# A graph kernel whose mean layers multiply by whole edge counts: rows scaled by their degree, one adjacency part instead of two

## The reference, cut to what matters

```python
cnt = segment_sum(ones, tgt); inv_cnt = 1.0 / maximum(cnt, 1.0)
for i in range(3):                       # the three mean layers with a norm
    x_in = x
    agg = segment_sum(x[src], tgt) * inv_cnt[:, None]
    h = agg @ W_l[i].T + x @ W_r[i].T + b[i]
    h = (h - mean(h)) * rsqrt(var(h) + 1e-5) * ln_g[i] + ln_b[i]
    x = relu(h) + x_in
...
h = agg / maximum(deg, 1.0)[:, None] @ W_l + b + x @ W_r      # the last mean layer
out = layernorm(x + h * sigmoid(h))
```

## Time and profile before

| | |
|---|---|
| median of 3 runs | 1023.49 us (1018.66 to 1024.08) |
| profiled execution | 1026.04 us, span from first to last instruction 1024.3 us |
| PE busy | 875.0 us (85%) |
| DVE busy | 692.1 us (68%) |
| ACT busy | 499.2 us (49%) |
| POOL busy | 333.7 us (33%) |
| mean layers 0 to 2 in the span | about 287 to 470 us |
| last mean layer and end | about 945 to 1024 us |

### The profile page before, as it was taken

How to read it: one execution, slowest core, us unless ns; L and a number is a source line. 1 busy time by engine, 2 the same in 40 slices (tenths; PEclk the granted TensorE clock), 3 DMA queues, 4 the chain that set the end, 5 groups by cost and what they waited for, 6 DMA issues and landing times.

```text
span 1024.3 us, 13343 instructions
## 1 busy us (share of the span) xinstructions
PE 875.0 (85%) x3642; PEld 624.8 (61%) x3642; DVE 692.1 (68%) x1228; ACT 499.2 (49%) x966; POOL 333.7 (33%) x286
## 2 busy tenths in 40 slices
PE   3979768678969999974999998999999988999793
PEld 2666245456747777753666765676655865667572
DVE  7997635576964646476887577964898569875414
ACT  2386004344534313345775566754776467743421
POOL 3000724567011123335360255503652064502100
PEclk9989557898969999996999999999999999999897
DMA  4413525878314130414683177812886058721001
GB/s 104 143 32 95 140 77 164 247 206 273 132 42 173 40 114 0 135 62 107 164 202 86 37 180 188 218 42 64 187 221 191 4 142 217 196 55 42 1 1 50
DMA packets 58198, 122.16 MB, mean 119 GB/s; under 512 B 8025, under 2 KB 21627, under 8 KB 58134
## 3 DMA queue, kind: packets, MB, share of 16 engines
q0 software_dynamic: 20048, 52.18, 21.5%
q1 hardware_dynamic: 35061, 63.82, 20.2%
q10 hardware_dynamic: 3024, 5.31, 1.4%
HBM read 105.56 MB, written 15.73 MB: 118 GB/s over the span
## 4 chain that ended last, share of the span: by engine, by line
PE 71%; DVE 16%; ACT 5%; issue 4%; DMA 1%; another core or an unknown queue 1%; SPq 0%; DVEq 0%; ACTq 0%
PE ps L908 14%; PE ps L653 12%; PE ps L885 10%; PE ps L924 6%; PE ps L940 6%; PE ps L847 5%; PE ps L796 5%; PE ps L772 4%; PE ps L755 2%; DVE z_parts L1581 2%; ACT slot_recs L995 2%; PE ps L744 1%; PE ps L645 1%; PE ps L659 1%; PE ps L679 1%
## 5 line engine op out<-in xcount | busy, mean ns | idle before, releaser
L908 PE MATMUL ps<-z_parts,onehot_dst 128*125 128x512 f32 x664 | 207.5, 418 | 12.6 <-DVE z_parts L1581 9.5
L653 PE MATMUL ps<-w,xT 128*125 128x512 f32 x660 | 175.0, 419 | 12.7 <-DVE w L1224 4.9
L1581 DVE SCALAR_TENSOR_TENSOR z_parts<-ps,z_parts 128x512 fp32r<-128x512 f32 x216 | 147.6, 687 | 50.8 <-ACT z_parts L1124 43.3
L1124 ACT ACTIVATE z_parts<-ps 128x512 fp32r<-128x512 f32 x216 | 129.1, 598 | 87.5 <-PE ps L885 78.1
L885 PE MATMUL ps<-x_parts,gather_lhs 128*128 x432 | 143.9, 419 | 32.1 <-DVE x_parts L1558 21.0
L908 PEld LDWEIGHTS ps<-z_parts,onehot_dst 128*125 128x125 f32 x664 | 111.6, 188 | 81.4 <-issue 63.0
L653 PEld LDWEIGHTS ps<-w,xT 128*125 128x125 f32 x660 | 126.5, 197 | 49.2 <-issue 19.9
L604 POOL DMA_INDIRECT gathered<-rel_rows,rowi x83 | 88.6, 1068 | 161.3 <-DMA rel_rows<-x_cur 96.1
L619 POOL DMA_INDIRECT queued<-node_rows,srci x60 | 96.1, 1601 | 104.0 <-ACT queued L1058 88.2
L885 PEld LDWEIGHTS ps<-x_parts,gather_lhs 128*128 128x128 f32 x432 | 81.4, 195 | 65.8 <-issue 48.9
L584 POOL TENSOR_TENSOR w<-w_stage,w 128x512 fp32r<-128x512 f32 x36 | 47.9, 1360 | 179.4 <-ACT w L957 179.4
(11 more groups left out here) (240 smaller groups left out, 1204.1 us busy)
## 6 DMA issues: line engine op xcount, KB each, us to landing
w_stage<-in_weights SPq DMA_DIRECT2D x22, 1024.0 KB
onehot_dst<-onehot_rows SPq DMA_DIRECT2D x80, 250.0 KB
onehot_rows<-onehot_dst ACTq DMA_DIRECT2D x20, 250.0 KB
gather_lhs<-edge_src_rows SPq DMA_DIRECT2D x8, 432.0 KB, 8.6
node_rows<-work SPq DMA_DIRECT2D x20, 160.0 KB, 2.0
queued<-node_rows,srci POOLq DMA_INDIRECT x116
node_rows<-work SPq DMA_DIRECT2D x20, 90.0 KB, 2.0
rel_rows<-rel_rows_out SPq DMA_DIRECT2D x10, 160.0 KB, 1.9
```

The lines of the kernel that those rows point to most:

```text
L653: mm = pe.matmul(ps[0:R, bank, :], lt[:, a, k, n * R:(n + 1) * R], w[:, b, k, :], start=first and k == 0 and (a, b) == THREE[0], stop=last ...
L908: mm = pe.matmul(ps[0:R, d, :], S[:, j // SK % SR, j % SK, :], Z[:, g % ZR, a, :], start=False, stop=False, skip_group_check=True)
L1124: nc.scalar.activation(Z[:, g % ZR, HI, :], of, ACT.Relu).then_inc(z_hi, 1)
L1581: v.scalar_tensor_tensor(out=Z[:, g % ZR, LO, :], in0=of, scalar=0.0, in1=Z[:, g % ZR, HI, :].bitcast(F32), op0=ALU.max, op1=ALU.subtract) ...
```

## The change

The mean layers are computed times their degree. With d the degree of a row (at least 1), d * h = counts @ (x W_l) + (d * x) W_r + d * b.

- **Counts stay whole numbers.** The kernel takes them as exact in the high part up to 4096, so `mean_tile` has two products per source tile instead of three: 10 instead of 15. The multiplication of the counts by the reciprocal is gone.
- **Two blocks keep a low part.** At most 2 of the 25 blocks of 125 by 125 can hold a count above 4096. DVE, PE and ACT look for the largest entry of each block (`block_max`, `block_row`, a chain of 13 small DVE operations), PE copies the low parts of the two blocks found, from an address in a register, to `CLO` (`low_blocks`), and each mean layer adds two products with them, with source and destination tile from registers (`mean_low`).
- **x is multiplied by its degree** on ACT ahead of the transposes (`by_degree`, one per tile, rows of `x_cur` into `work`, counted by `xd_made`). The rows `x @ W_l` come out multiplied too, so `y_high` and `y_low` take the reciprocal as a factor. The roots take `eps * d^2`.
- **The bias** is multiplied by the degree: five products with four rows of degree parts (`DGR`, `deg_rows` in the trace) behind all `z_tile`s (`z_bias`), instead of one with two rows of ones ahead of each.
- **Degrees** are summed to one column per tile (25 products of one column instead of 10 of 313 or 312), and `deg_made` comes within the second round of DVE's first norm.
- **Places.** `DGR` shares its memory with the rows `WEB`, so SP stores it, waits for the third layer's `z_bias`, then loads `WEB` (`web_load(0)`) and only then weight 13 (`w_load(13)`); the first five `queue_set`s move behind `w_highs(9 + 2 * l)` on ACT.

```diff
@@ PE @@
             def x_tile(l, n):
-                pe.wait_ge(x_made, XM_MEAN[l] + n + 1)
-                transposes(n, X[0:R, n, :])
+                pe.wait_ge(xd_made, NT * l + n + 1)
+                transposes(n, H[0:R, n, :])
...
             def z_tile(l, n):
-                bias(n, k)
-                mm = natural(n, XT, W[1], n, first=False, last=False)
+                mm = natural(n, XT, W[1], n, last=False)
...
+            def z_bias(l):
+                k = l if l < NL1 else NL1 + NL2
+                pe.wait_ge(bias_in[k % 2], 32 * (k // 2 + 1))
+                if l == NL1:
+                    pe.wait_ge(dgr_in, 16)
+                else:
+                    pe.wait_ge(dgr_made, 1)
+                for n in range(NT):
+                    mm = pe.matmul(ps[0:R, n, :], DGR[:, n * R:(n + 1) * R], BIAS[:, k % 2, :],
+                                   start=False, stop=False)
+                mm.then_inc(zb_done, 1)
...
+            def low_blocks():
+                pe.wait_ge(low_made, 3)
+                pe.wait_ge(at_made, NT)
+                for j in range(2):
+                    wd = low_word(j)
+                    b = field(wd, 6, 31, NB - 1)
+                    mm = pe.matmul(ps[0:R, 5, P * (j + 1):P * (j + 1) + R], ident[0:R, 0:R],
+                                   ATL[0:R, bass.ds(b * R, R)], start=True, stop=True)
+                mm.then_inc(low_done, 1)
...
+            def mean_low(l):
+                if l == 0:
+                    pe.wait_ge(clo_made, 1)
+                pe.wait_ge(y_out, Y_L1[l] + NT)
+                for j in range(2):
+                    wd = low_word(j)
+                    s = field(wd, 0, 7, NT - 1)
+                    d = field(wd, 3, 7, NT - 1)
+                    pe.matmul(psf[0:R, bass.ds(d * D, D)], CLO[0:R, j, :], XS[0:R, HI, bass.ds(s, 1), :],
+                              start=False, stop=False, skip_group_check=True)
+
             def mean_tile(l, n):
...
                 for s in range(NT):
-                    for a, b in THREE:
-                        mm = pe.matmul(ps[0:R, n, :], AT[0:R, a, s, n * R:(n + 1) * R], XS[0:R, b, s, :],
-                                       start=False, stop=s == NT - 1 and (a, b) == THREE[-1])
+                    for b in (HI, LO):
+                        mm = pe.matmul(ps[0:R, n, :], AT[0:R, HI, s, n * R:(n + 1) * R], XS[0:R, b, s, :],
+                                       start=False, stop=s == NT - 1 and b == LO)
                 mm.then_inc(o_done, 1)
...
                 for n in range(NT):
                     z_tile(l, n)
+                    if l == 0 and n < NT - 1:
+                        (lambda: None, deg_rows, block_max, block_row)[n]()
+                    if l == 0 and n == NT - 2:
+                        low_blocks()
+                z_bias(l)
+                mean_low(l)
@@ ACT @@
+            def by_degree(n, count):
+                act.wait_ge(x_made, count)
+                nc.scalar.activation(H[0:R, n, :], X[0:R, n, :], ACT.Copy, scale=degp[0:R, n:n + 1])\
+                    .then_inc(xd_made, 1)
...
                 if l == 0:
                     for s in range(NT):
-                        act.wait_ge(an_made, s + 1)
                         nc.scalar.copy(AT[:, HI, s, :], TC[:, s, :]).then_inc(at_hi, 1)
...
+                    act.wait_ge(low_done, 3)
+                    nc.scalar.copy(CLO[0:R, :, :], ps[0:R, 5, P:3 * P].rearrange("p (j n) -> p j n", n=P)[:, :, 0:R])\
+                        .then_inc(clo_made, 1)
                 w_highs(8 + 2 * l)
+                act.wait_ge(z_done, l + 1)
+                w_highs(9 + 2 * l)
                 if l == NL1 - 1:
                     for k in range(0, EARLY, 2):
                         queue_set(0, k)
-                act.wait_ge(z_done, l + 1)
-                w_highs(9 + 2 * l)
                 if l < NL1 - 1:
-                    for n in range(NT + 1):
+                    for n in range(NT + 2):
                         if n < NT:
-                            root(n, NT * (l + 1) + n + 1)
+                            root(n, NT * (l + 1) + n + 1, epsd)
                             normal(H[0:R, n, :], ps[0:R, n, :], n, NT * (l + 1) + n + 1, h_made)
-                        if n >= 3:
+                        if n >= 2:
+                            by_degree(n - 2, XM_L1[l + 1] + n - 1)
+                        if 3 <= n <= NT:
                             tr_high(n - 3, XT, n - 3, TR_L1[l + 1] + n - 2)
@@ SP @@
+            sp.wait_ge(dgr_made, 1)
+            sp.dma_start(dg_d, DGR[:, :].bitcast(F32)).then_inc(dgr_out, 16)
+            sp.wait_ge(zb_done, NL1)
+            sp.wait_ge(dgr_out, 16)
+            web_load(0)
             w_load(13)
```

More of the change, by code:

```diff
@@ L418, in bias_load @@
             def bias_load(k, row):
-                sp.dma_start(BIAS[:, k % 2, :].bitcast(F32), rw_d[:, row, :]).then_inc(bias_in[k % 2], 16)
+                for i in (0, 2):
+                    sp.dma_start(BIAS[i:i + 2, k % 2, :].bitcast(F32), rw_d[:, row, :]).then_inc(bias_in[k % 2], 16)
             def ln_load(l):
@@ new lines, in deg_rows, with block_max @@
+            def deg_rows():
+                pe.wait_ge(y_out, 4)
+                for n in range(NT):
+                    mm = pe.transpose(ps[0:4, 7, n * R:(n + 1) * R] if n < 4 else ps[0:4, 5, 0:R],
+                                      DG4[0:R, n, :], ident[0:R, 0:R])
+                mm.then_inc(dgr_tr, 1)
+            def block_max():
+                pe.wait_ge(y_out, NT)
+                pe.wait_ge(low_made, 1)
+                pe.transpose(ps[0:NB, 6, 0:R], bm[0:R, :], ident[0:R, 0:R]).then_inc(low_done, 1)
@@ L961, in w_highs, with root @@
                     w_high(j, k)
-            def root(n, count):
+            def root(n, count, eps=None):
                 act.wait_ge(ln_var, count)
-                nc.scalar.activation(sd[0:R, n:n + 1], mv[0:R, n, 1:2], ACT.Sqrt, bias=epst[0:R, 0:1])\
+                nc.scalar.activation(sd[0:R, n:n + 1], mv[0:R, n, 1:2], ACT.Sqrt,
+                                     bias=epst[0:R, 0:1] if eps is None else eps[0:R, n:n + 1])\
                     .then_inc(ln_sd, 1)
@@ L974, in y_high @@
                 act.wait_ge(y_done, NREL * NT + count)
-                nc.scalar.copy(XS[0:R, HI, n, :], ps[0:R, bank, :]).then_inc(y_hi, 1)
+                nc.scalar.activation(XS[0:R, HI, n, :], ps[0:R, bank, :], ACT.Copy, scale=rdegp[0:R, n:n + 1])\
+                    .then_inc(y_hi, 1)
+            def by_degree(n, count):
+                act.wait_ge(x_made, count)
+                nc.scalar.activation(H[0:R, n, :], X[0:R, n, :], ACT.Copy, scale=degp[0:R, n:n + 1])\
+                    .then_inc(xd_made, 1)
             act.wait_ge(edges_in, 64)
@@ L1047, in _ @@
                     normal(X[0:R, n - 1, :], H[0:R, n - 1, :], n - 1, n, x_made)
+                    act.wait_ge(deg_made, 1)
+                    by_degree(n - 1, n)
                 if 2 <= n < NT:
@@ L1167, in _ @@
                 normal(X[0:R, n, :], H[0:R, n, :], n, NT * (NL1 + 2) + n + 1, x_made)
+                by_degree(n, XM_L3 + n + 1)
                 if n >= 2:
@@ L1177, in _ @@
                 act.wait_ge(o_done, NT * NL1 + n + 1)
-                nc.scalar.activation(X[0:R, n, :], ps[0:R, n, :], ACT.Sigmoid).then_inc(sg_out, 1)
+                nc.scalar.activation(X[0:R, n, :], ps[0:R, n, :], ACT.Sigmoid, scale=rdegp[0:R, n:n + 1])\
+                    .then_inc(sg_out, 1)
             for n in range(NT):
```

124 lines of the change are left out of this document (93 added, 31 removed).

## The result

The changed kernel takes **1053.55 us** as a median of 4 runs (1051.44 to 1056.19), the kernel before 1023.78 beside it: ratio 1.0288, 95% interval [1.0235, 1.0340]. The forecast was 1057, with a range of 1036 to 1070. The profiled execution took 1051.44 us with a span of 1049.6, 25.3 longer than that of before; PE is busy 859.7 us instead of 875.0, DVE 692.3 and ACT 515.9. So PE has 15 us less work and the program takes longer: the time went into waits.

The account below looks back on a forecast made before the run. The prediction took PE's in-order path from a layer's first root to the next layer's first product as the bound, not the products. Its terms, 1.2 + 1 + 9.4 + 11.3 + 10.1 + 4 - 3.6 = +33.4, gave 1057 us, range 1036 to 1070.

Parts of the forecast that it names:

- What bounds it: Layer 0: PE and DVE nearly level from tile 2; PE's 13.9 us from first root to next layer's first product matters.
- Head of layer 0, +1: Before layer 0's z tiles: degree sums, small DVE operations and by_degree cost more than the saved reciprocal wait; +1 us (-3 to +5).
- Search and weight 9, +9.4: Layer 0, z tiles to first root: the block search delays w_highs(8) and weight 9's load; root at 31.0, +9.4 us.
- The ring, +11.3 and +10.1: Layers 0 and 1: x_tile(n - 2) waits on tile n's products through DVE and ACT, closing a chain; +11.3 and +10.1 us.
- my 4: Layers 0 and 1: loss per layer from PE's lower clock after waits, 4 us taken between bounds 0 and 8.6.
- Layer 2, +4: Layer 2: weight 13 loads only after z_bias, delaying ACT's queue_sets and root; +4 us.
- Last mean layer, -3.6: Last mean layer: by_degree adds 0.9 us, but fewer products let tile 4 start earlier at the end; -3.6 us.
- z_bias and mean_low, +1.2 over the layers: Mean layers: z_bias saves about 1.0 us a layer, mean_low adds 1.4; +0.4 each, +1.2 for three layers.
- products bound it: Rival: PE sets the pace throughout, so cutting products makes the kernel faster, 1002 us; chance 7 in 100.
- every burst is cold: Rival: every product burst runs at the lower clock, 1066 us, or 1070 with a colder block search; chance 15 in 100.
- the search and weight 9 hide: Rival: only the loops, layer 2 and the tail count and the clock stays full; about 1040 us, chance 15 in 100.
- gains and losses cancel: Rival: one closed loop costs less and the search hides; within 5 us of 1023, chance 5 in 100.

Follow-up runs that it names:

- the cut alone: The kernel before with two products per source tile instead of three in all four mean layers, nothing else changed: 981.35 us, ratio 0.9924.
- the version that hides the search: The kernel with the three edits, with layer 0's head reordered and the block search moved into existing waits: 978.34 us, ratio 0.9859 to the kernel before.
- the head's reordering: The kernel with the three edits, with DVE's statistics of tiles 0 to 3 ahead of its degree wait and transpose copies one round later: 980.22 us, ratio 0.9887.
- closed alone in the kernel before: The kernel before, with PE in layers 0 and 1 waiting for tile n's normal ahead of tile n - 2's transposes: 1012.78 us, ratio 1.0237.
- the kernel with weight 13 early: The changed kernel, with SP issuing weight 13's load ahead of its wait for the third z_bias: 1052.74 us, ratio 1.0328 to the kernel before.
- the opened kernels: Changed kernels with by_degree of tile n - 2 ahead of root and normal of tile n in layers 0 and 1; that edit alone: 1030.47 us, ratio 1.0105.
- the kernel with the three edits: The changed kernel with by_degree ahead of root and normal, weight 8's split and low_blocks reordered, weight 13 loaded early: 1015.9 us, ratio 0.9981.

## Why the prediction was right, by its steps

- **What bounds it.** "A shorter product tile can pay little there" held: the cut alone is worth 7.5 us in the total and 11.0 by stages, of 23.1.
- **Head of layer 0, +1.** Measured +0.1, which is partly luck. The degree products went from 7.2 to 9.3 us, +2.1 where I took +2.3. But the first y tile came 7.1 us later (22.7 behind the first b_self product, before 15.6), where my added terms make 5.2, and 7.0 were made up between it and the z tiles, where I took 4.46: the second y tile now ran in 3.02 us instead of 5.32. The head also hid a cost that I did not see as one. Its rounds, 5.35 us from root to root (4.54 before), are themselves a ring, and reordering them was worth 6.4.
- **Search and weight 9, +9.4.** Measured +9.2; the root came at 30.8 for 31.0. The chain was as worked out: z tile 4 and `w_highs(8)` behind the search, then the load (ACT waited 8.85). But when that order was undone 5 to 6.5 came back, not 9.4. The rest stays with the added products on PE, which in the version that hides the search doesn't wait for DVE there and still needs 19.0 from the z tiles to the adjacency products, 16.7 before. Counted from b_self, that version's products start 4.0 us sooner than before, the head's reordering included.
- **The ring, +11.3 and +10.1.** Measured +11.8 and +10.1. Shown from both sides: opened, it gives 12.9 instead of 25.4; closed alone in the kernel before, it costs 13.7 and 10.7. Of the two parts in layer 1, the 21.2 us at full clock are 25.4 - 4.1 = 21.3. The clock's part is mis-sized: my 4 stood for two bursts, their transposes and the y tile together, and those lost 4.1 up to y and 1.5 in the y tile, 5.6. The bound of 8.6, every burst at 0.50 from end to end, was not reached, since only one of a layer's two bursts ran so. The Trainium skill, page "TensorE: Matmul & The Clock Gate", section "HAM oscillation — how this bites in real kernels", says that in a loop of short bursts with waits between them each burst starts at the lower clock. This trace agrees, more than I allowed for: in both layers each burst and the y tile began at 0.50, the first behind waits of 8.13 and 4.70 us, the others behind 3.40. Layer 0's first rounds hold one more part that I did not have: from the root to the statistics of tile 2 it took 5.3 us (4.4 in layer 1, 4.25 forecast). There POOL's work on the late weight 9 (350.30 to 355.72) lies over DVE's norm, and DVE's `nmr` took 0.62 and 0.91 us instead of 0.16.
- **Layer 2, +4.** Measured +4.9: statistics of tile 1 at 12.2 instead of 11.4, since the rows `WEB` went ahead of the weight in the queue (6.5 us from issue to split for 5.3), which I had named and priced at 1. The edit gave 4.7 back. The 2.6 that the wait for `WEB` and the queue rows still holds are not in the prediction's sum.
- **Last mean layer, -3.6.** Measured -5.5. The end behind the first adjacency product is 5.0 shorter (4.55 forecast), the head 0.8 longer (0.9), DVE's tiles 2.31 apart (2.28). The rest, -1.2, is the next term.
- **z_bias and mean_low, +1.2 over the layers: mis-sized, even in sign.** I took 1.43 for `z_bias` and 1.4 for `mean_low`; in layer 2 of the kernel with weight 13 early the two took 1.9 together (470.27 to the adjacency products at 472.17). There `mean_low` started 0.35 us late, and only once. (In layer 0 of the opened kernels its second product was 0.41 late as well.) From a layer's y to its first adjacency product the kernel with the three edits takes 31.4 us, before 32.5: -1.1 a layer instead of +0.4. In the changed kernel the y tile at the lower clock ate most of it (32.2). So the clock term was 1.5 too small and this one 1.5 too large, and that the stages from y to y came out right is luck to that extent.
- **Sum.** +30.6 in the stages touched, against 33.4. As measured (medians), the change cost 29.8. Of the rivals, "products bound it" is refuted by the cut alone, and "every burst is cold" by the clock's 5.6 of 8.6. That the search and weight 9 hide, and that gains and losses cancel, are refuted by the stages.

## What to carry to other kernels

On in-order engines a new step between two engines is placed by what stands ahead of it in each program, not by what it needs: for each wait that moves to another engine, write down the last instruction ahead of the signal there, and follow it back. If it comes from work that stands behind the wait, the engines take turns, and a round costs the sum of their parts instead of the longest one (6.4 us here even at the full clock, 4.0 before). Check it in the order of instructions, before anything runs: here two lines in another order were worth 19 of 30 us. And where a total is noisier than the edit, read the stage between two instructions of its own, and keep an untouched stage beside it as a measure of the noise.
